# Four attention and ffn layers on one core: a new SBUF plan, ffn chunks placed beside attention slots, and the first attention pieces placed inside the ffn

## The reference

```
x = L0_attn_hidden_states
for each layer L:
    xn = layernorm(x)
    s = attention_L(xn)          # 32 heads of 16; layers 0, 2, 3: 8 kv heads, rope, causal; layer 1: 32 kv heads, no mask
    g = silu(ffn_L(xn))
    x = x + s * g
# ffn 0: silu(xn Wg) * (xn Wu), then Wd; octonion ternary weights, hidden 1366
# ffn 1: xn W + bias, W unpacked from int4
# ffn 2: silu(xn W1) * (xn W3), then W2, weights scaled by block, hidden 1792
# ffn 3: ((silu(gate) * up) U2) V2 + b2 with gate, up from (xn U1) V1 + b1, hidden 1376, rank 128
```

## Time and profile before

| what | us |
|---|---|
| median of 3 runs | 1371.65 (1370.09 to 1372.38) |
| the profiled execution | 1376.63 |
| its span in the trace | 1374.9 |
| TensorE busy in it | 1233.0 (90%) |
| VectorE, ScalarE, GpSimd busy | 796.6, 667.7, 379.6 |

### The profile page before, as it was taken

How to read it: one execution, slowest core, us unless ns; L and a number is a source line. 1 busy time by engine, 2 the same in 40 slices (tenths; PEclk the granted TensorE clock), 3 DMA queues, 4 the chain that set the end, 5 groups by cost and what they waited for, 6 DMA issues and landing times.

```text
span 1374.9 us, 22607 instructions
## 1 busy us (share of the span) xinstructions
PE 1233.0 (90%) x8860; PEld 918.3 (67%) x8860; DVE 796.6 (58%) x1311; ACT 667.7 (49%) x1114; POOL 379.6 (28%) x460
## 2 busy tenths in 40 slices
PE   4999989999999899877889999979899889898897
PEld 3888867665665555545668888867667666676574
DVE  7743557755566565745355556466676767665243
ACT  3433346555465456765033343246665655556453
POOL 1000324323211000012244444234432343434242
PEclk9999979999999999889999999979999999999897
DMA  7000000110001000010333223110001000010001
GB/s 276 1 1 0 1 2 3 47 56 2 1 2 35 1 2 1 25 47 24 104 103 99 92 92 95 43 47 3 1 2 39 2 2 33 2 45 2 1 16 46
DMA packets 15260, 48.07 MB, mean 35 GB/s; under 512 B 2859, under 2 KB 6960, under 8 KB 14389
## 3 DMA queue, kind: packets, MB, share of 16 engines
q1 hardware_dynamic: 15156, 46.63, 9.9%
HBM read 44.00 MB, written 2.10 MB: 34 GB/s over the span
## 4 chain that ended last, share of the span: by engine, by line
PE 72%; DVE 12%; ACT 9%; issue 4%; DMA 1%; POOL 0%; SPq 0%; POOLq 0%; DVEq 0%; ACTq 0%
PE bank L622 19%; PE bank L738 13%; PE bank L652 9%; PE bank L876 8%; PE bank L836 6%; PE bank L784 4%; ACT probs L1242 4%; DVE negmax L1611 3%; PE bank L752 3%; PE bank L816 2%; PE bank L847 2%; ACT pv L1250 2%; PE bank L764 1%; PE bank L793 1%; PE bank L855 1%
## 5 line engine op out<-in xcount | busy, mean ns | idle before, releaser
L1611 DVE TENSOR_REDUCE negmax<-bank 128x4 f32<-128x1024 f32 (+1 forms) x256 | 249.5, 1017 | 73.0 <-PE bank L793 57.4
L1242 ACT ACTIVATE probs<-bank 128x1024 f32<-128x1024 f32 (+1 forms) x256 | 216.6, 865 | 51.9 <-PE bank L816 44.2
L1828 POOL TENSOR_SCALAR_AFFINE_SELECT probs<-probs 128x512 f32<-128x512 f32 x192 | 124.5, 658 | 304.1 <-ACT probs L1242 304.1
L1771 POOL TENSOR_TENSOR W_lo<-W_lo_whole,W_hi 128x1536 fp32r<-128x1536 f32 x28 | 98.1, 3502 | 134.5 <-ACT W_hi L1049 134.5
L784 PE MATMUL bank<-kT,qT 64*128 64x256 f32 (+1 forms) x1024 | 109.5, 312 | 23.8 <-DVE negmaxT L1629 6.9
L836 PE MATMUL bank<-probs,V 128*32 128x256 f32 (+1 forms) x2048 | 121.1, 355 | 6.2 <-DVE negmax L1611 2.5
L1250 ACT ACTIVATE pv<-bank 128x256 f32<-128x256 f32 x128 | 49.2, 385 | 157.8 <-PE bank L836 157.5
L816 PE MATMUL bank<-qT,kT 64*128 64x256 f32 (+1 forms) x640 | 115.4, 389 | 5.0 <-DMA qT<-negmaxT 2.0
L784 PEld LDWEIGHTS bank<-kT,qT 64*128 64x128 f32 x1024 | 84.5, 197 | 51.9 <-issue 30.6
L1049 ACT ACTIVATE W_hi<-W_lo_whole 128x1536 fp32r<-128x1536 f32 x28 | 41.7, 1488 | 139.9 <-DVE W_lo_whole L1455 139.9
L622 PE MATMUL bank<-xT_hi,W_hi 128*128 128x512 f32 x224 | 88.9, 397 | 10.3 <-DVE xT_lo L1349 5.7
(11 more groups left out here) (194 smaller groups left out, 2729.5 us busy)
## 6 DMA issues: line engine op xcount, KB each, us to landing
W_lo_whole<-in_w SPq DMA_DIRECT2D x28, 768.0 KB, 4.2
Wqkv_lo_whole<-in_Wqkv SPq DMA_DIRECT2D x6, 768.0 KB, 6.4
Wo_lo_whole<-in_Wo SPq DMA_DIRECT2D x4, 1024.0 KB, 6.6
Wqkv<-in_Wqkv SPq DMA_DIRECT2D x2, 1536.0 KB, 7.6
Wdown_whole<-in_Wd SPq DMA_DIRECT2D x1, 2816.0 KB, 14.1
x<-in_x SPq DMA_DIRECT2D x4, 512.0 KB, 5.4
out<-x SPq DMA_DIRECT2D x8, 256.0 KB, 2.0
V_lo_whole<-in_V SPq DMA_DIRECT2D x1, 1408.0 KB, 6.1
```

Of the source, the lines that this page charges most:

```text
L1242: nc.scalar.activation(A[l].probs[gi % 2][kb][:, :, q0 - kb * A[l].probs1:].rearrange("p (b h) q -> p b h q", b=2), B.tensor(key)[:, :, 0: ...
L1611: v.tensor_reduce(A[l].negmax[u % 2][:, qb, :].rearrange("p (b h) -> p b h", b=2)[:, :, 2 * g:2 * g + 2], B.tensor(key)[:, :, 0:2 * nk].re ...
L1771: gp.tensor_tensor(lo, whole, hi.bitcast(F32), ALU.subtract).then_inc(w_low.sem, 1)
L1828: gp.affine_select(out=blk, in_=blk, compare_op=ALU.is_ge, fill=0.0, base=0, pattern=[[0, 4], [1, P]], channel_multiplier=-1).then_inc(cau ...
```

## The change

Five things are changed together; the text of the silu operations is the same before and after (one activation each, in both kernels).

1. **Memory plan.** Buffers in SBUF are placed anew (Wo, the W2 buffers, the stacks of layers 0 and 1, qT and kT), so that weights and chunks of ffn2 and ffn3 can be in place while attention still runs. Wo of layer 0 is now loaded after the last out tile of ffn0, Wo of layer 2 after chunk 25 of ffn2, and both are cut into parts in unit 1 of their run.
2. **PSUM.** In ffn0 and ffn2 all chunks use banks 0 and 1 (before: 0, 1 and 2, 3 in turn), which frees banks 2 and 3. `tile1` uses bank 0 (once bank 1).
3. **Start of attention inside the ffn.** `first_rows` is gone. The first projections, stacks and rows of scores stand between the last chunks of ffn0 and ffn2.
4. **Ffn chunks inside the run.** Chunks 0 and 1 of ffn2 stand in (14, 3) to (15, 2) of run 0, halves at a time, and chunks 0 to 6 of ffn3 in seven slots of run 1, from (14, 1) to (15, 3).
5. **Layer 1's ffn earlier.** `unpack` is cut in five, from (6, 1) to (7, 3); `tile1` stands in (10, 3) to (13, 0); its result is gated as the others are.

```diff
-HBUFS = 5
+HBUFS = {0: 4, 2: 4, 3: 5}
-TILE1_SLOTS = {(13, 0): 0, (13, 1): 1, (13, 3): 2, (14, 1): 3, (14, 2): 4, (14, 3): 5, (15, 0): 6, (15, 1): 7}
+UNPACK_SLOTS = {(6, 1): 0, (6, 3): 1, (7, 0): 2, (7, 1): 3, (7, 3): 4}
+TILE1_SLOTS = {(10, 3): 0, (11, 0): 1, (11, 1): 2, (11, 3): 3, (12, 0): 4, (12, 1): 5, (12, 3): 6, (13, 0): 7}
+TURN2_SLOTS = {(13, 1): 0, (13, 3): 1, (14, 1): 2, (14, 2): 3}
+WEIGHTS2_SLOTS = {(13, 2): 0, (14, 2): 1, (15, 1): 2}
+PART2_SLOTS = {(14, 3): (0, 0), (15, 0): (0, 1), (15, 1): (1, 0), (15, 2): (1, 1)}
+HIDDEN2_SLOTS = {(15, 0): 0, (15, 2): 1}
+CHUNKS2_EARLY = 2
+CHUNK3_SLOTS = {(14, 1): 0, (14, 2): 1, (14, 3): 2, (15, 0): 3, (15, 1): 4, (15, 2): 5, (15, 3): 6}
+CHUNKS3_EARLY = 7
...
             def ffn0():
-                for e in range(2 * HC0):
-                    gate_up(0, e, 2 * (e % 2))
...
+                C = 2 * HC0
+                for e in range(C):
+                    half_chunk(0, e, 0, 0)
+                    if e == C - 1:
+                        turn_queries(0, 0, 0, 2)
+                    half_chunk(0, e, 1, 0)
+                    if e == 1:
+                        weight_sum(2)
+                    if e == C - 5:
+                        project(0, 0, 0, bank=2)
+                    if e == C - 4:
+                        project(0, 0, 1, bank=3)
+                    if e == C - 3:
+                        project(0, 1, 0, bank=2)
+                    if e == C - 2:
+                        project(0, 1, 1, bank=3)
+                    if e >= LAG[0]:
+                        down(0, e - LAG[0])
+                turn_keys(0, 0, 0, 0)
+                turn_queries(0, 0, 1, 2)
+                turn_keys(0, 0, 1, 1)
+                down(0, C - 3)
+                scores_rows(0, 0, 0, (0, 2))
+                scores_rows(0, 0, 1, (2, 2))
+                down(0, C - 2)
...
             def ffn2():
+                weigh_values(0, last, last)
+                turn_context(0, last - 1, last)
+                transposes(2, (4, 5), banks=(2, 3))
+                for e in range(CHUNKS2_EARLY, C):
+                    half_chunk(2, e, 0, 0)
...
+                    if C - 4 <= e < C - 1:
+                        scores_rows(1, (3 * (e - C + 4)) // 2, (3 * (e - C + 4)) % 2, (2, 2))
...
             def ffn2():
+                for e in range(CHUNKS2_EARLY, C):
+                    if e > CHUNKS2_EARLY and e + 2 < C:
                         weights_high(e + 2)
                     hidden(2, e)
...
-            load(Wo_whole[:], a["Wo0"], wo_in)
+            sp.wait_ge(*B.filled(("out", 0, TILES - 1)))
+            load(Wo_whole[0][:], a["Wo0"], wo_in)
...
+            sp.wait_ge(*chunk_used(2, 2 * HC2 - 3))
+            load(Wo_whole[1][:], a["Wo2"], wo_in)
```

More of the change, by code:

```diff
@@ L416, in program @@
         assert at[0] <= R + 102496
-        at = [R + first["ctxT_lo"]]
-        silu1 = [place(f"silu1_{i}", [P, D], F32, at) for i in range(2)]
         at = [R + 102496]
@@ L423, in program @@
         assert at[0] <= SBUF_END
-        at = [R]
         W2_hi, W2_whole, W2_lo = [], [], []
-        for i in range(W2BUFS):
+        for i, start in enumerate((WA + 12288, WP, R, R + 12288)):
+            at = [start]
             W2_hi.append(place(f"W2_hi{i}", [P, 3 * KC, P], F32R, at))
@@ L589, in gate_up, with half_chunk @@
             def gate_up(l, e, bank):
+                for which in range(2):
+                    half_chunk(l, e, which, bank)
+            def half_chunk(l, e, which, bank):
                 n, j = divmod(e, HIDDEN_CHUNKS[l])
                 tok = slice(n * 512, (n + 1) * 512)
-                if l != 3 and j == 0:
-                    for t in range(4 * n, 4 * n + 4):
-                        pe.wait_ge(*B.emptied(("xT", l, t)))
-                if l == 0 and n == 0:
-                    pe.wait_ge(*tern_ready.at(0, need_gate_up[j]))
-                    if j == HC0 - 1:
-                        pe.wait_ge(*padding_set.at(0, 2))
@@ new lines, in half_chunk @@
+                if which == 0:
+                    if l != 3 and j == 0:
+                        for t in range(4 * n, 4 * n + 4):
+                            pe.wait_ge(*B.emptied(("xT", l, t)))
+                    if l == 0 and n == 0:
+                        pe.wait_ge(*tern_ready.at(0, need_gate_up[j]))
+                        if j == HC0 - 1:
+                            pe.wait_ge(*padding_set.at(0, 2))
+                    if l == 2:
+                        pe.wait_ge(*w_low.at(2, e + 1))
+                    if l == 3 and j == 0:
+                        pe.wait_ge(*B.emptied(("low", n)))
+                    if l == 3 and n == 0 and j % 4 == 0:
+                        pe.wait_ge(*w_low.at(3, 4 + j // 4))
@@ new lines, in half_chunk @@
+                key = (("gate", "up")[which], l, n, j)
+                ps = claim(key, bank + which)
+                terms = []
+                for c in range(KC):
+                    hi, lo = xT_hi[:, c, tok], xT_lo[:, c, tok]
+                    if l == 0:
+                        w = W0[which][:, c, j * P:(j + 1) * P]
+                        terms += [(w, hi), (w, lo)]
+                    if l == 2:
+                        w = W2_hi[e % W2BUFS][:, KC * which + c, :]
+                        terms += [(w, hi), (w, lo), (W2_lo[e % W2BUFS][:, KC * which + c, :], hi)]
@@ L625, in down @@
+                if l == 3:
+                    w = W3_hi["V1"][:, which, j, :]
+                    terms = [(w, PT_hi[n][:]), (w, PT_lo[n][:]), (W3_lo["V1"][:, which, j, :], PT_hi[n][:])]
+                for c, (lh, rh) in enumerate(terms):
+                    ins = mm(ps[:], lh, rh, start=(c == 0), stop=(c == len(terms) - 1))
+                ins.then_inc(B.fills(key), 1)
             def down(l, e):
@@ L910, in slot @@
                     filled_out = True
-                if r == 0 and (U, g) in TILE1_SLOTS:
-                    tile1(TILE1_SLOTS[U, g])
+                if r == 0 and (U, g) in PART2_SLOTS:
+                    e, which = PART2_SLOTS[U, g]
+                    half_chunk(2, e, which, 0)
                     filled_out = True
@@ L941, in ffn0 @@
                     if e >= LAG[0]:
                         down(0, e - LAG[0])
-                first = [(0, 0), (0, 1), (1, 0)]
-                for i, e in enumerate(range(2 * HC0 - LAG[0], 2 * HC0)):
-                    down(0, e)
-                    project(0, *first[i], bank=i)
-                project(0, 1, 1, bank=3)
+                turn_keys(0, 0, 0, 0)
[3 more added lines that the diff above has]
+                scores_rows(0, 0, 0, (0, 2))
@@ L949, in ffn2 @@
+                turn_stacks(0, 1, 0)
+                scores_rows(0, GROUPS, 0, (4, 2))
+                scores_rows(0, GROUPS, 1, (0, 2))
             def ffn2():
                 last = RUN * GROUPS - 1
-                for e in range(2 * HC2):
-                    gate_up(2, e, 2 * (e % 2))
-                    if e == 0:
-                        weigh_values(0, last, last)
-                        turn_context(0, last - 1, last)
-                        transposes(2, (4, 5), banks=(2, 3))
-                    if e == 1:
+                C = 2 * HC2
@@ L1006, in _ @@
             ffn0()
-            first_rows(0)
             for G in range(RUN * GROUPS):
```

579 lines of the change are left out of this document (323 added, 256 removed).

## The result

| kernel | median us | range | runs |
|---|---|---|---|
| before | 1370.18 | 1362.62 to 1376.96 | 20 |
| after | 1375.43 | 1371.97 to 1388.43 | 20 |

The ratio of after to before is 1.0044, with a 95% interval of 1.0025 to 1.0062: the change makes the kernel about 6 us slower. The forecast was 1335. The profiled execution of before lies some 6 us above the median of these runs and the one of after at its median, so the two traces, of 1374.9 and 1374.4 us, are nearly equal: what they explain is why 36.9 us did not come, and less why 6 were lost.

A forecast was written before the change was run, and what follows sets the result against it. TensorE, busy 1233 of 1374.9 us, was taken as the bound, so only its idle or slow time could be won. Gains less losses summed to 36.9 us, taking the median from 1371.65 to about 1335, range 1312 to 1356.

The forecast's parts named there:

- The tiles now stand beside long projections, where ScalarE has time for them: Units 11 to 15 of run 0: 26.4 of 31.4 us lost would be left, so 5.0 us won.
- Starts of the two runs: Projections, stacks and scores among the last ffn chunks shorten TensorE's waits: 11.5 us won after ffn0, 10.6 after ffn2.
- Start of ffn2: Head of ffn2: a wait for GpSimd's `W_lo` goes, a stop of about 5 us at gate half 4 comes; 12.7 us won.
- One pair of banks: Ffn0 and ffn2: gate halves must wait for the previous chunk's silu; 2.4 us lost in ffn0, 1.5 in ffn2's body.
- The second rival: The single bank pair ties ffn2 to its loads, deciding from 1.5 us per chunk; 1378 us at 1.8; chance 0.07.
- Unit 10: Unit 10 of run 0: unpacking cut in five and put where VectorE has room; 5.5 us won.
- End of run 1: Slots with ffn3 chunks, units 14 and 15 of the second attention: ScalarE becomes the bound at 5.7 us a slot; 3.5 lost.
- signs of being wrong: Ffn2 period clearly over 8.3 us, last attention slots over 7, 1.2 GHz in units 11 to 13, or unchanged start waits.
- Wo cut inside unit 1: Unit 1 of each attention run: GpSimd's cutting of Wo now stands behind the causal cuts; 1.0 us lost.
- Lost us: TensorE's measure for a stretch: length less busy time, plus length times 1 less the clock; 114.6 us at the touched places.
- case 3: Rival: table switches in slots cost twice their row, 1355 us; with a milder slow-clock case, 5 to 22 won, chance 0.15.

The follow-up runs named there:

- run 0: Not a follow-up: the kernel's own stretch of attention between ffn0 and ffn2; its first slot starts at 182.6 us before the change, 175.7 after.
- the copies: The change with every silu that stands in an attention slot replaced by a copy, so no table is loaded there; ratio to before 0.9875.
- the last kernel: The change with two bank pairs, early stacks, unpacking moved, tiles spread, no early ffn2 or ffn3 chunks, and a one-column exponential behind each tile's silu; 1331.58 us, ratio 0.9721.
- that kernel: The change with the second stack of the attention after ffn2, unit 0, made one step earlier on both ScalarE and GpSimd; ratio to before 0.9998.

## Why the prediction was wrong

**Where it failed.** The step that failed first is "The tiles now stand beside long projections, where ScalarE has time for them", with "Left: 6.4% of 157.3, 10, plus 14.4, plus 2". The price of a switch was near (1.3 us of waiting and 0.5 of clock for each tile forecast; 1.84 of waiting measured in most tile slots, and by the copies 1.4 in all for each silu). What I left out is that the slots which the tiles leave do not shrink by a tile: units 13 and 14 had waited for ScalarE beside their tiles, and without them TensorE waits at `weigh_values` instead (6.7 us), and at `scores_rows` for the bank of the turned rows (3.4 us). I took the ordinary 6.4% for all slots that had no tile. I had read the 8.1 us in four waits of the earlier trace rows as waits of the tile's banks, which bank 0 would end; after, TensorE waits 6.7 us in four for the same exponentials, at `weigh_values`. The wait was the slot's, and the tile had only stood where it shows. Units 11 to 15 left 43.5 us lost where the sum says 26.4. The run with the tiles spread again, 10 us faster, shows that the early place costs; why it does stays partly open, since the waits behind the exponentials hardly differ between the two places (21.3 and 22.2 us) and the slow clock does (30.7 and 20.5). What cuts these waits, by half, is taking the tables away (9.6 us) or loading the exponentials' table ahead of the copy of `pv` (10.9 us in the last kernel); moving the tiles left them as they were.

**Starts of the two runs.** For run 0 the mechanism was right, and the size nearly: first slot at 175.7, forecast near 178. But unit 0 stayed at the low clock (0.77) where "unit 0 is mostly at full clock" was forecast. For run 1, "I leave 8.5 of 19.1: 10.6 won" failed for two reasons. First, a wait of 4.46 us that I had not found: I had followed banks and row maxima, but not what stands *ahead* of `stack_high` and `stack_low` on ScalarE and GpSimd, the weights of chunk C-4 with the wait for their load. The chain in after:

```profile
855.12 1.49 ACT L1117 ACTIVATE W_hi<-W_lo_whole 128x1536 fp32r<-128x1536 f32 x1 [7.90 <-DVE W_lo_whole L1547]
...
858.39 0.61 ACT L1319 ACTIVATE qstack<-rope_cos 128x512 fp32r<-128x512 f32 x1
...
861.24 0.56 POOL L1930 TENSOR_TENSOR kstack<-rope_cos,kstack 128x64 fp32r<-128x64 f32 x1
...
862.08 0.72 PE L772 MATMUL bank<-ident_r,qstack 128*128 128x128 f32 x4 [4.46 <-POOL kstack L1930]
```

Second, I counted only idle and slow time. With the stop gone the eight chunks still take 97.3 us, where the lost time fell by about 7 us from before and the length by 2.7: TensorE's busy time at full clock rose from 88.4 us (its 92.32, less half of the 7.8 busy us at the low clock) to 91.3. The same matmuls cost 3 us more in the new order. A part of it can be seen: the twelve matmuls of a half chunk start within 2.49 us in the old order, and within 2.58 to 2.65 us in most half chunks of that kernel from chunk 23 on, where groups of scores and turnings stand between them; the first takes 0.30 to 0.34 us and not 0.23. Over fifteen of the sixteen half chunks that is some 1.2 us; the sixteenth ran partly at the low clock. The rest is not located.

**Start of ffn2.** Right: 9.6 won, forecast 12.7, with the stop of TensorE at gate half 4 behind silu (4.9 us) as foretold.

**One pair of banks.** "The slack is nil. I add 0.1 us for each of some 15 chunks" was three times too small: 0.31 a chunk, and with ffn0 and the stop at gate half 4 the run with two pairs was 6 us faster. In ffn0 the 2.4 us forecast came as a wait of 2.0 us. The second rival was the right mechanism at a fifth of its deciding price.

**Unit 10.** 5.5 forecast; the slot (10, 2) fell from 10.9 to 5.1 us, so what was to be won there was won. But (7, 0) rose from 7.3 to 10.4: `unpack`'s 2 us stand ahead of the row maxima there too. What this is worth in run time stays open, since moving the piece gave nothing. Most of the rest that the ledger shows for units 7 to 10 is moved work: the four `group_values` stood in units 11 and 12 before and stand in units 8 and 9 now (after falls back 3.3 us over these two), and the first tile stands in (10, 3), which takes 3.0 us more. This work came out of units 11 to 15, which lost so much more than their 6.1 us. That (10, 0) takes 1.2 us more is not explained.

**End of run 1.** 3.5 lost was forecast, 9 measured (by the run without the chunks, whose interval reaches from 5 to 14). The slot (14, 3), forecast 10.3, took 14.5 us: one of the signs of being wrong that the prediction names (over 7 us). Two more came: a period of ffn2's chunks over 8.3 us (8.47), and stretches at 1.2 GHz in units 11 to 13 (17 us of them in after).

**Wo cut inside unit 1.** No run isolates the 1.0 lost. From the first slot to unit 3, after falls back by 0.7 us in run 0 and wins 0.7 in run 1.

**The sum.** Lost us were priced alike, idle or slow, at half a microsecond for each at the low clock. Traces of kernels that are the same up to the place give less or equal: from unit 11 to the end of unit 15, 32.7 slow us in after against 25.9 with two bank pairs made 174.3 against 171.0 us (0.5 each); in the first three units of run 1, 10.2 slow with the copies against 0 in after made 61.8 against 58.8 (0.3); in ffn3's end 18.4 with GpSimd's stack moved against 1.3 in after made 72.9 against 66.8 (0.36).

**The rivals.** I gave "slower" 0.07, for one mechanism. What came was none of the cases: mid-sized losses, of 6 to 10 us each by the runs (single bank pair 6, stacks 6, ffn3's chunks 9, early tiles 10), in places where I had put gains or small losses. The table, case 3, was right in its direction: the Trainium skill, page "ScalarE: Activation LUTs", section "What ACT_TABLE_LOAD costs", puts a price on every switch, and 23 us went with the switches. The price of the load, 1.28 us, agrees with the traces. But its 1.38 us of drain is not the reason: in both timelines the next activation starts 0.01 to 0.02 us after the load's end. The loss is the place of the load in ScalarE's order, behind a copy that waits for TensorE.

## What to carry to other kernels

When work is moved to fill idle time, ask two questions about the place that it leaves: what did this work cover there, and who takes the wait now. Here the waits behind the exponentials were 18.8 to 22.2 us wherever the tiles stood, and only taking the table loads away, or moving them, made them shorter. For each moved piece, read what stands ahead of it on *every* engine that it passes, above all a wait for a load, which is free for its own consumer and dear for a guest behind it. And undo parts singly before giving up on a change: this one lost 0.4% as a whole, and with its start of attention kept, its early chunks, early tiles and single bank pair taken out, and a table load moved, it is 2.8% faster than the kernel before.
